# A perceiver layer on one core: the last 65 keys spread over four row groups, loaded by four transfers from ScalarE

## The chip, the core and the metric

The kernel runs on one core of a Trainium2 chip. Five engines work side by side: TensorE (PE; PEld is its weight load), VectorE (DVE), ScalarE (ACT), GpSimd (POOL) and SyncE (SP, which here only issues transfers). Each has a stream of its own, and they wait for each other by semaphores. Transfers issued on SP or on ScalarE are carried out by 16 DMA engines that all queues share. The metric is the device time of one execution in microseconds (us); lower is better.

## The reference, cut to what matters

The layer has three parts: cross-attention, a small self-attention, and a mixture of experts. The change touches the first alone. There are 32 batches with 64 queries each, a context of 1601 keys, and 256 channels, all in fp32.

```python
q = jnp.einsum('bsd,df->bsf', query, Wq) + bq       # query: x, normed; (32, 64, 256)
k = jnp.einsum('bsd,df->bsf', key_in, Wk) + bk      # key_in = value = ctx_1024; (32, 1601, 256)
v = jnp.einsum('bsd,df->bsf', value, Wv) + bv
attn = jnp.einsum('bqd,bkd->bqk', q, k)
probs = jax.nn.softmax(attn, axis=-1)
result = jnp.einsum('bqk,bkd->bqd', probs, v)
x = result + query                                  # then a layer norm with gamma and beta
```

## The kernel before, in words

The weights of queries and keys are multiplied ahead, so that scores come straight from the context. Two batches make a pair (128 query rows), and 16 pairs are worked through. The context of a pair lies in one of three slots of `ring`, as 12 chunks of 128 keys and a 13th chunk with the rest. 1601 is 12 x 128 + 65, and the 65 lie on partitions 0 to 64 of chunk 12 (`KT` is 12, `TAIL` 65, `Q` 32, `QUADS` 4).

For each pair VectorE turns the keys in blocks of 32 x 32 (L1714, eight column blocks of 128x832, into `ctxT`). Thus partitions 32a to 32a+31 hold the keys of row group a, for 32 channels. A row group's keys over the 13 chunks are `KW[a]` many: 416, 416, 385, 384. TensorE then makes the scores (`scores`, L1180): for each of 8 column blocks and 4 row groups and 2 batches a matmul with 32 rows, 64 columns and `KW[a]` moving columns, into bank a of `S`. An fp32 matmul leaves two records. VectorE takes the maximum over each bank (L1726), ScalarE the exponentials (`exps`, L901: five instructions, as `EXPS` lists the whole blocks of 32 and the odd column apart) with their sums. TensorE turns the probabilities chunk by chunk (`turn_probs`, L1194) in the parts `KPARTS`, chunks 0-3, 4-7, 8-11 and 12, into four banks; ScalarE copies each part (`turned_out`, L888); TensorE weighs the context with them (`weigh`, L1206).

In `turn(i)` TensorE does the scores of pair i, turns pair i-2's result, weighs pair i-1, projects pair i-2 and turns pair i's probabilities. ScalarE does the copies of pair i-1 first, then what belongs to pairs i-2 and i-3, then the exponentials of pair i. VectorE does the maxima of pair i, five column blocks of pair i+1, sums and residual, and the last three column blocks.

All loads of the context stand on SP (`load_part`, L439 for three transfers of four chunks, 1 MB each, L443 for the rest, 130 KB). `follow(i, r)` waits for the scores and, part by part, for the weighing of pair i-3, with a store of an older pair's result and the load of pair i's queries (`load_q`, L452) around it. VectorE begins a pair when all its transfers have landed (`ctx_loaded[r]`). ScalarE's own queue carries two loads of x, two bias vectors, and `store_q` (L861) three times. GpSimd zeroes chunk 12 of each slot at the start (`tails_ready`), and SP waits for it ahead of the first load. Bank 0 holds scores and then, from column 0 on, the first part of the turned probabilities.

Of the kernel before, what the change touches and what calls it, by code (L numbers as in the profile page):

```python
# [6 lines left out]
def perceiver_layer(nc, t, out):  # L7
# [9 lines left out]
    NL, NB, D = x_in.shape  # L17
# [64 lines left out]
    with cross:  # L82
# [85 lines left out]
        sums = sb("sums", [P, len(EXPS)])  # L168
# [258 lines left out]
        def _(sp):  # L427
# [6 lines left out]
            def load_part(i, r, g, loaded=None):  # L434

                pair = ctx_in[bass.ds(2 * i, 2)]
                ks = KPARTS[g]
                if ks[0] < KT:
                    sp.dma_start(ring[:, r, :, ks[0]:ks[-1] + 1, :].rearrange("p b k c -> p b (k c)"),  # L439
                                 pair[:, 0:KT * P, :].rearrange("b (p k) c -> p b k c", k=KT)[:, :, ks[0]:ks[-1] + 1, :]  # L440
                                 .rearrange("p b k c -> p b (k c)")).then_inc(loaded or ctx_loaded[r], 16)
# [30 lines left out]
            sp.wait_ge(tails_ready, RING)  # L472
# [342 lines left out]
        def _(act):  # L815
            for n in range(2):
                part = slice(*XPARTS[n])
                act.dma_start(x_all[:, part, :], x_rows[:, part, :]).then_inc(x_loaded[n], 16)
# [3 lines left out]
                          allow_slow_non_contiguous=True).then_inc(qkb_loaded, 16)  # L822
            act.wait_ge(wT_done, 1)
# [56 lines left out]
            queries_placed(0)  # L880
            queries_placed(1)

            def turned_out(i):

                for g, ks in enumerate(KPARTS):
                    rows = P if ks[0] < KT else TAIL
                    act.wait_ge(probT_done, i * len(KPARTS) + (g + 1))
                    act.copy(probT[0:rows, ks[0]:ks[-1] + 1, :].rearrange("p a b -> p (a b)"),  # L888
                             PT_BANKS[g][0:rows, 0:len(ks) * P]).then_inc(probT_copied, 1)

            def exps(i):
# [3 lines left out]
                for n, (a, lo, hi) in enumerate(EXPS):  # L895
                    if hi - lo >= Q:
                        to = by_slab[:, lo // Q:hi // Q, a, :]
                        of = S[a][:, lo:hi].rearrange("p (k j) -> p k j", j=Q)
                    else:
                        to, of = by_slab[:, lo // Q, a, 0:hi - lo], S[a][:, lo:hi]  # L900
                    act.activation(to, of, ACT.Exp, bias=negmax[:, 0:1], accum_out=sums[:, n:n + 1]).then_inc(exp_done, 1)  # L901
# [18 lines left out]
            def turn(i, ahead=True, back1=True, back2=True, back3=True, rows=None, queries=None):  # L920

                if back1:
                    turned_out(i - 1)
                if rows:
# [18 lines left out]
            turn(2, back3=False, queries=1)  # L943
            store_q(1)
            turn(3, rows=2)
            turn(4, queries=2)
            store_q(2)
            turn(5, rows=3)
            turn(6, queries=3)
            store_q(3)  # L950
            with act.Fori(7, PAIRS) as i:
                turn(i)
# [123 lines left out]
        def _(pe):  # L1076
# [107 lines left out]
            def turn_probs(i, first=False, turned=None):  # L1184

                pe.wait_ge(exp_done, (i + 1) * len(EXPS))
                for g, ks in enumerate(KPARTS):
# [4 lines left out]
                    for a, k in enumerate(ks):  # L1192
                        rows = P if k < KT else TAIL
                        last = pe.transpose(PT_BANKS[g][0:rows, a * P:a * P + P], prob[:, k * P:k * P + rows], ident[:, :])  # L1194
# [1059 lines left out]
```

## Time and profile before

| | |
|---|---|
| median of 3 runs | 530.31 us (527.97 to 533.57) |
| profiled execution | 530.5 us, span 528.3 us |
| TensorE busy | 493.6 us (93%) |
| VectorE busy | 387.4 us (73%) |
| ScalarE busy | 219.3 us (42%) |
| GpSimd busy | 203.6 us (39%) |
| granted TensorE clock | 0.985 of full speed |
| DMA moved | 108.92 MB, mean 206 GB/s |

The busy times say how long an engine had an instruction of its own running; DMA issues and waits are not in them. The attention stage is the first half of the span. The chain of waits follows the work back from the last instruction. The timeline lists instructions merged in groups, with the idle time ahead of a group in brackets and who ended it.

### The profile page before, as it was taken

How to read it: one execution, taken by the hardware profiler on the slowest of the kernel's cores; microseconds unless marked ns; L12 is line 12 of the kernel's file. 1: busy time of each engine (PE TensorE's matmuls, PEld its weight loads, DVE VectorE, ACT ScalarE, POOL GpSimd, SP SyncE). 2: the span in 40 equal slices, each digit the busy share in tenths (PEclk: the TensorE clock that was granted, in tenths of full speed). 3: DMA queues.
4: the chain of work that ended last, by engine and by line, in shares of the span. 5: the costliest groups of instructions: out<-in, count | busy, mean ns of one | idle time of the engine just before them, and what ended most of it. 6: DMA issues, size and time to landing. Idle time of an engine off the chain costs nothing.

```text
span 528.3 us, 14495 instructions
## 1 busy us (share of the span) xinstructions
PE 493.6 (93%) x5028; PEld 345.8 (65%) x5029; DVE 387.4 (73%) x1053; ACT 219.3 (42%) x656; POOL 203.6 (39%) x344
## 2 busy tenths in 40 slices
PE   7999999899999999999989999999988879999990
PEld 6766566565666666666655577767745658888870
DVE  4887896998788889898543588889776415555764
ACT  3344443353333434444331466656431025555510
POOL 5000422121222111222231577776676605566640
PEclk9999999999999999999999999999999979999996
DMA  7998979966989988884215999710122234555747
GB/s 287 358 342 296 224 229 301 330 212 176 323 293 299 308 292 285 292 270 133 58 41 154 274 321 299 206 51 2 45 88 82 90 100 143 164 160 149 231 107 232
DMA packets 67610, 108.92 MB, mean 206 GB/s; under 512 B 8371, under 2 KB 49381, under 8 KB 67560
## 3 DMA queue, kind: packets, MB, share of 16 engines
q1 hardware_dynamic: 60872, 97.57, 58.8%
q0 software_dynamic: 3792, 8.43, 4.6%
q10 hardware_dynamic: 2896, 2.23, 1.3%
q8 instruction: 33, 0.54, 0.5%
q14 instruction: 17, 0.14, 0.1%
HBM read 85.31 MB, written 24.85 MB: 209 GB/s over the span
## 4 chain that ended last, share of the span: by engine, by line
PE 75%; DVE 6%; DMA 6%; POOL 6%; issue 3%; ACT 2%; ACTq 1%; SPq 1%; POOLq 0%; DVEq 0%
PE banks L1206 16%; PE banks L1180 16%; PE banks L1590 8%; POOL rows_by_expert L773 4%; PE banks L1602 4%; PE banks L1194 3%; PE banks L1219 2%; DMA ring<-in_ctx_dram 2%; PE banks L1584 2%; PE banks L1317 2%; PE banks L1369 2%; PE banks L1227 2%; PE banks L1324 2%; PE banks L1340 1%; PE banks L1149 1%
## 5 line engine op out<-in xcount | busy, mean ns | idle before, releaser
L1714 DVE STREAM_TRANSPOSE ctxT<-ring 128x832 f32<-128x832 f32 x124 | 118.2, 1010 | 6.3 <-DMA ring<-in_ctx_dram 6.0
L1180 PE MATMUL banks<-ctxT,qT_all 32*64 32x416 f32 (+2 forms) x2048 | 94.4, 498 | 2.8 <-DVE ctxT L1714 1.5
L1206 PE MATMUL banks<-ring,prob 128*64 128x256 f32 (+1 forms) x832 | 93.6, 381 | 0.7 <-ACT prob L888 0.7
L1206 PEld LDWEIGHTS banks<-ring,prob 128*64 128x64 f32 (+1 forms) x832 | 58.7, 137 | 31.5 <-issue 4.2
L1180 PEld LDWEIGHTS banks<-ctxT,qT_all 32*64 32x64 f32 x2048 | 55.5, 131 | 33.1 <-issue 11.4
L672 POOL TENSOR_TENSOR var<-mv,eps 128x1 f32<-128x1 f32 x32 | 6.1, 191 | 147.6 <-DVE mv L1755 93.4
L807 POOL DMA_INDIRECT expert_out<-prob,dest x47 | 46.2, 983 | 41.1 <-issue 21.7
L1590 PE MATMUL banks<-ring,ctxT 128*128 x188 | 50.4, 392 | 0.1
L901 ACT ACTIVATE prob<-banks,negmax 128x416 f32<-128x416 f32 (+2 forms) x80 | 40.9, 531 | 19.8 <-DVE negmax L1736 19.8
L1726 DVE TENSOR_REDUCE blockmax<-banks 128x1 f32<-128x416 f32 (+1 forms) x64 | 32.3, 567 | 16.6 <-PE banks L1180 16.6
L720 POOL TENSOR_TENSOR ctxT<-ctxT,k_mask 128x1088 f32<-128x1088 f32 x16 | 33.1, 2068 | 24.9 <-ACT ctxT L997 24.9
L2169 DVE TENSOR_TENSOR ctxT<-banks,ctxT 128x128 f32<-128x128 f32 x47 | 13.7, 292 | 32.7 <-ACT ctxT L1058 32.5
L1590 PEld LDWEIGHTS banks<-ring,ctxT 128*128 128x128 f32 x188 | 33.3, 198 | 3.3 <-issue 0.5
L888 ACT COPY prob<-banks 128x512 f32<-128x512 f32 x64 | 27.5, 515 | 16.7 <-PE banks L1194 16.6
L1602 PE MATMUL banks<-ring,ctxT 128*128 x94 | 28.0, 381 | 0.0
L1194 PE MATMUL banks<-ident,prob 128*128 128x128 f32 (+1 forms) x208 | 25.6, 273 | 1.2 <-ACT turned L843 0.7
L918 ACT COPY UT<-banks 128x256 f32<-128x256 f32 x16 | 6.0, 374 | 48.8 <-PE banks L1213 48.8
L1194 PEld LDWEIGHTS banks<-ident,prob 128*128 128x128 f32 (+1 forms) x208 | 23.5, 140 | 3.3 <-ACT turned L843 1.0
L2176 DVE TENSOR_SCALAR prob<-banks,share 128x256 f32<-128x256 f32 x47 | 22.6, 480 | 1.5 <-PE banks L1602 0.8
L1058 ACT ACTIVATE ctxT<-banks 128x128 f32<-128x128 f32 x47 | 13.0, 277 | 23.5 <-PE banks L1590 23.5
L1584 PE MATMUL banks<-ident,ctxT 128*128 128x128 f32 x94 | 18.8, 285 | 3.7 <-DMA ctxT<-rows_by_expert 3.7
L691 POOL TENSOR_TENSOR xn_all<-xn_all,bv_b 128x256 f32<-128x256 f32 (+1 forms) x16 | 11.8, 738 | 22.3 <-DMA rbias_b<-n_L_ffn_router_bias_dram 20.5
(279 smaller groups left out, 947.6 us busy)
## 6 DMA issues: line engine op xcount, KB each, us to landing
ring<-in_ctx_dram SPq DMA_DIRECT2D x48, 1024.0 KB, 8.8
qT_all<-q_by_pair SPq DMA_DIRECT2D x56, 128.0 KB, 8.2
rows_by_expert<-blank SPq DMA_DIRECT2D x8, 774.0 KB, 5.8
ctxT<-rows_by_expert SPq DMA_DIRECT2D x47, 129.0 KB, 2.1
mid<-stage SPq DMA_DIRECT2D x30, 128.0 KB, 2.3
ring<-in_ctx_dram SPq DMA_DIRECT2D x16, 130.0 KB
ctxT<-mid SPq DMA_DIRECT2D x16, 128.0 KB, 3.5
qT_all<-mid SPq DMA_DIRECT2D x16, 128.0 KB, 4.4
```

Source lines behind the costliest of these rows:

```text
L720: pool.tensor_tensor(k_blk, k_T.unsqueeze(2).broadcast_to([P, GB, HEADS, NP]), k_mask[:, :].unsqueeze(1).unsqueeze(3).broadcast_to([P, GB, ...
L807: pool.indirect_dma_start(y_dram, bass.IndirectOffsetOnAxis(ap=dest[:, s:s + 1], axis=0), y_sb[:, r, :], None, bounds_check=TOPK * TOK - 1 ...
L888: act.copy(probT[0:rows, ks[0]:ks[-1] + 1, :].rearrange("p a b -> p (a b)"), PT_BANKS[g][0:rows, 0:len(ks) * P]).then_inc(probT_copied, 1)
L901: act.activation(to, of, ACT.Exp, bias=negmax[:, 0:1], accum_out=sums[:, n:n + 1]).then_inc(exp_done, 1)
L1180: last = pe.matmul(S[a][64 * b:64 * b + 64, 0:KW[a]], q_rep[mine, r, c, 64 * b:64 * b + 64], ctxT[mine, c, b, 0:KW[a]], start=c == 0, stop ...
L1194: last = pe.transpose(PT_BANKS[g][0:rows, a * P:a * P + P], prob[:, k * P:k * P + rows], ident[:, :])
L1206: last = pe.matmul(U[64 * b:64 * b + 64, 0:D], probT[0:rows, k, 64 * b:64 * b + 64], ring[0:rows, r, b, k, :], start=k == 0, stop=k == KT)
L1584: last = pe.transpose(bank[r % 2][:, dh * P:dh * P + P], row_in[:, r, dh * P:dh * P + P], ident[:, :])
L1590: last = pe.matmul(bank[2 + p][:, 0:2 * HID], rowT[:, p, k, :], w_gu[:, bass.ds(e, 1), k, :].squeeze(1), start=k == 0, stop=k == DH - 1)
L1602: pe.matmul(bank[6 + p][:, 0:D], hidT[:, p, :], w_down[:, bass.ds(e, 1), :].squeeze(1), start=True, stop=True)\
L1714: dve.transpose(ctxT[:, c].rearrange("p b (k j) -> p (b k) j", j=Q), ring[:, r].rearrange("p b k c -> p (b k) c")[:, :, columns(c):columns ...
L1726: dve.tensor_reduce(blockmax[:, a:a + 1], S[a][:, 0:KW[a]], AX.X, ALU.max).then_inc(blockmax_ready, 1)
```

## The change

The 65 keys of chunk 12 are spread 17, 16, 16, 16 over the four row groups (`TAILS`), each group's from partition 32a on, so that `KW` becomes 401, 400, 400, 400. Four transfers bring them, and they are issued on ScalarE by `load_rest`, one turn ahead of their use and behind the copies of `turned_out`. SP's four transfers now hold chunks 0-2, 3-6, 7-10 and 11. The exponentials become four, each over all 416 columns of its bank; the columns from `KW[a]` on hold -1e30, written once by VectorE, so their exponentials are zero. `KPARTS` becomes 3, 4, 4 and 2 chunks, which keeps the first part in bank 0 off these columns. The turned and weighed last chunk has 128 rows instead of 65. SP no longer waits for `tails_ready`; ScalarE does. The loop on ScalarE has three turns in its body instead of one.

```diff
-    KW = [KT * Q + max(0, min(Q, TAIL - Q * a)) for a in range(QUADS)]
-    EXPS = [(a, lo, hi) for a in range(QUADS) for lo, hi in ((0, KW[a] // Q * Q), (KW[a] // Q * Q, KW[a])) if lo < hi]
-    KG = 4
+    TAILS = [TAIL // QUADS + (1 if a < TAIL % QUADS else 0) for a in range(QUADS)]
+    KW = [KT * Q + n for n in TAILS]
+    NEVER = -1e30
...
-    KPARTS = [range(lo, min(lo + KG, KT + 1)) for lo in range(0, KT + 1, KG)]
+    KPARTS = [range(0, 3), range(3, 7), range(7, 11), range(11, KT + 1)]
+    CTX_LOADS = 16 * (len(KPARTS) + QUADS)
...
-                ks = KPARTS[g]
-                if ks[0] < KT:
-                    sp.dma_start(ring[:, r, :, ks[0]:ks[-1] + 1, :].rearrange("p b k c -> p b (k c)"),
...
-                else:
-                    sp.dma_start(ring[0:TAIL, r, :, KT, :],
-                                 pair[:, KT * P:KEYS, :].rearrange("b p c -> p b c")).then_inc(ctx_loaded[r], 16)
+                lo, hi = KPARTS[g][0], min(KPARTS[g][-1] + 1, KT)
+                sp.dma_start(ring[:, r, :, lo:hi, :].rearrange("p b k c -> p b (k c)"),
...
-            sp.wait_ge(tails_ready, RING)
...
+            def load_rest(i, r):
+
+                pair = ctx_in[bass.ds(2 * i, 2)]
+                for a, n in enumerate(TAILS):
+                    at = KT * P + sum(TAILS[:a])
+                    act.dma_start(ring[Q * a:Q * a + n, r, :, KT, :],
+                                  pair[:, at:at + n, :].rearrange("b p c -> p b c")).then_inc(ctx_loaded[r], 16)
...
+            act.wait_ge(tails_ready, RING)
+            load_rest(0, 0)
...
             queries_placed(0)
+            for i in range(1, RING):
+                load_rest(i, i)
             queries_placed(1)
...
-                for n, (a, lo, hi) in enumerate(EXPS):
...
+                for a in range(QUADS):
+                    act.activation(by_slab[:, :, a, :], S[a][:, 0:SLAB].rearrange("p (k j) -> p k j", j=Q), ACT.Exp,
+                                   bias=negmax[:, 0:1], accum_out=sums[:, a:a + 1]).then_inc(exp_done, 1)
...
                 if back1:
                     turned_out(i - 1)
+                if rest is not None:
+                    load_rest(i + 1, rest)
...
-            with act.Fori(7, PAIRS) as i:
-                turn(i)
+            turn(7, rest=2)
+            turn(8, rest=0)
+            with act.Fori(3, PAIRS // RING) as it:
+                for u in range(RING):
+                    turn(it * RING + u, rest=(u + 1) % RING)
+            turn(PAIRS - 1)
...
-            dve.wait_ge(ctx_loaded[0], 64)
+            dve.wait_ge(bk_row_copied, 1)
+            for a in range(QUADS):
+                dve.memset(S[a][:, KW[a]:SLAB], NEVER)
+            dve.wait_ge(ctx_loaded[0], CTX_LOADS)
             for c in range(SOONER):
                 chunks_turned(c, arrived, KT + 1).then_inc(block_ready, 1)
             for c in range(SOONER, BLOCKS):
                 block_turned(0, 0, c, 0)
-            dve.wait_ge(bk_row_copied, 1)
```

On ScalarE, one turn in the body of the loop stood like this before (`prob` is written in its second half, `probT`, by the copies; ISA and REGISTER_ALU set addresses and counts):

```order
L888 COPY prob<-banks 128x512
L887 REGISTER_ALU
L888 COPY prob<-banks 65x128
L918 COPY UT<-banks 128x256
L911 ISA
L912 ACTIVATE stage<-stage,nmr,rstd 128x16x16
L893 REGISTER_ALU
L901 ACTIVATE prob,sums<-banks,negmax 128x13x32 x2
L901 ACTIVATE prob,sums<-banks,negmax 128x12x32
L901 ACTIVATE prob,sums<-banks,negmax 128x1
L901 ACTIVATE prob,sums<-banks,negmax 128x12x32
```

The same place of the changed program, from the last copy on:

```order
L895 COPY prob<-banks 128x256
L817 ISA
L817 DMA ring<-in_ctx_dram 17x2x256
L817 ISA
L817 DMA ring<-in_ctx_dram 16x2x256
L817 ISA
L817 DMA ring<-in_ctx_dram 16x2x256
L817 ISA
L817 DMA ring<-in_ctx_dram 16x2x256
L921 COPY UT<-banks 128x256
L914 ISA
L915 ACTIVATE stage<-stage,nmr,rstd 128x16x16
```

Four transfers now stand between the last copy and the work on the older pairs.

On VectorE, the first keys of pair 0 stood like this before:

```order
L1698 COPY prob<-w_mem 128x2x128 x2
L1815 STREAM_TRANSPOSE ctxT<-ring 128x2x256 x4
L1815 STREAM_TRANSPOSE ctxT<-ring 128x2x160 x4
L1714 STREAM_TRANSPOSE ctxT<-ring 128x832 x4
L1784 ISA dotted,shift<-xn_all,bk_row 128x256
```

And in the changed program:

```order
L1705 COPY prob<-w_mem 128x2x128 x2
L1822 STREAM_TRANSPOSE ctxT<-ring 128x2x224 x4
L1831 MEMSET banks 128x15
L1831 MEMSET banks 128x16 x3
L1822 STREAM_TRANSPOSE ctxT<-ring 128x2x192 x4
L1721 STREAM_TRANSPOSE ctxT<-ring 128x832 x4
L1791 ISA dotted,shift<-xn_all,bk_row 128x256
```

The first step turns seven chunks instead of eight, four fills have come in behind it, and the second step turns six instead of five.

## Rows read from the trace of the kernel before

**Rows 1.** Window table, 180 to 210 us; columns as in its head.

```profile
core 0: us, PE busy (x) PEld busy (x) DVE busy (x) ACT busy (x) POOL busy (x), PEclk, DMA share, GB/s
180.00:210.00 30.00, 30.00 (x442) 20.12 (x434) 27.17 (x55) 11.91 (x34) 6.55 (x16) 1.00 0.87 285
```

**Rows 2.** Chain of waits, one steady turn: start us, us, what.

```profile
177.94 5.75 PE banks L1180 x112
...
184.06 5.77 PE banks L1206 x52
...
192.31 5.75 PE banks L1180 x112
```

**Rows 3.** Chain of waits, the first six pairs.

```profile
17.48 6.40 PE banks L1180 x113
...
28.05 2.55 ACT prob L901 x10
...
63.78 0.57 ACTq L861
...
65.11 0.59 ACT prob L888
...
80.31 12.46 DMA ring<-in_ctx_dram
```

**Rows 4.** Timeline of a steady turn: start, us, engine, line, operation, [idle before, releaser].

```profile
186.86 3.10 SPq L439 DMA_DIRECT2D ring<-in_ctx_dram  x3
...
188.28 0.26 ACT L901 ACTIVATE prob<-banks,negmax 128x1 f32<-128x1 f32 x1
...
188.52 0.59 ACT L901 ACTIVATE prob<-banks,negmax 128x384 f32<-128x384 f32 x1
...
190.27 0.36 SPq L443 DMA_DIRECT2D ring<-in_ctx_dram  x1
...
191.36 1.71 ACT L888 COPY prob<-banks 128x512 f32<-128x512 f32 x4 [1.01 <-PE banks L1194]
...
192.24 5.82 PE L1180 MATMUL banks<-ctxT,qT_all 32*64 32x416 f32 x128
...
193.20 2.88 DVE L1714 STREAM_TRANSPOSE ctxT<-ring 128x832 f32<-128x832 f32 x3
...
198.19 2.02 DVE L1726 TENSOR_REDUCE blockmax<-banks 128x1 f32<-128x416 f32 x4 [0.99 <-PE banks L1180]
...
198.46 0.37 ACT L918 COPY UT<-banks 128x256 f32<-128x256 f32 x1 [5.38 <-PE banks L1213]
...
200.94 4.75 DVE L1714 STREAM_TRANSPOSE ctxT<-ring 128x832 f32<-128x832 f32 x5
```

**Rows 5.** Groups by line and shape, 192 to 199 us: busy us, mean ns.

```profile
L1180 PE MATMUL banks<-ctxT,qT_all 32*64 32x416 f32 x64 | 5.8, 510 | 0.0
L1180 PE MATMUL banks<-ctxT,qT_all 32*64 32x385 f32 x32 | 5.4, 485 | 0.0
L1180 PE MATMUL banks<-ctxT,qT_all 32*64 32x384 f32 x32 | 5.4, 484 | 0.0
```

**Rows 6.** Timeline of the start.

```profile
1.32 0.46 SPq L429 DMA_DIRECT2D ring<-in_L_xattn_Wk_dram  x1
...
2.29 1.40 SPq L439 DMA_DIRECT2D ring<-in_ctx_dram  x3
...
11.12 0.29 DVE L1701 COPY bk_rep<-bk_col 128x256 f32<-128x256 f32 x1 [1.91 <-DMA bk_col<-in_L_xattn_bk_dram]
...
16.33 1.69 DVE L1815 STREAM_TRANSPOSE ctxT<-ring 128x320 f32<-128x320 f32 x4 [0.47 <-DMA ring<-in_ctx_dram]
```

**Rows 7.** DMA issues: KB each, median us from issue to landing.

```profile
mid<-stage SPq DMA_DIRECT2D x30, 128.0 KB, 2.3
...
q_by_pair<-w_mem ACTq DMA_DIRECT2D x8, 128.0 KB, 7.8
...
q_by_pair<-qT_all ACTq DMA_DIRECT2D x4, 128.0 KB, 8.3
```

**Rows 8.** Timeline of TensorE, the scores of pair 5.

```profile
104.29 2.78 PE L1180 MATMUL banks<-ctxT,qT_all 32*64 32x416 f32 x48 [1.54 <-DVE ctxT L1714]
```

More of the change, by code:

```diff
@@ L167, in perceiver_layer @@
         negmax = sb("negmax", [P, 1])
[L168 removed]
+        sums = sb("sums", [P, QUADS])
         rowsum = sb("rowsum", [P, 1])
@@ L436, in load_part @@
                 pair = ctx_in[bass.ds(2 * i, 2)]
[L437 to L444 removed]
+                lo, hi = KPARTS[g][0], min(KPARTS[g][-1] + 1, KT)
+                sp.dma_start(ring[:, r, :, lo:hi, :].rearrange("p b k c -> p b (k c)"),
+                             pair[:, 0:KT * P, :].rearrange("b (p k) c -> p b k c", k=KT)[:, :, lo:hi, :]
+                             .rearrange("p b k c -> p b (k c)")).then_inc(loaded or ctx_loaded[r], 16)
             def load(i, r):
@@ L885, in turned_out @@
                 for g, ks in enumerate(KPARTS):
-                    rows = P if ks[0] < KT else TAIL
                     act.wait_ge(probT_done, i * len(KPARTS) + (g + 1))
-                    act.copy(probT[0:rows, ks[0]:ks[-1] + 1, :].rearrange("p a b -> p (a b)"),
-                             PT_BANKS[g][0:rows, 0:len(ks) * P]).then_inc(probT_copied, 1)
+                    act.copy(probT[:, ks[0]:ks[-1] + 1, :].rearrange("p a b -> p (a b)"),
+                             PT_BANKS[g][:, 0:len(ks) * P]).then_inc(probT_copied, 1)
             def exps(i):
@@ L918, in UT_evac, with turn @@
                 act.copy(UT[:, :, :].rearrange("p a b -> p (a b)"), M[:, 0:D]).then_inc(UT_copied, 1)
-            def turn(i, ahead=True, back1=True, back2=True, back3=True, rows=None, queries=None):
+            def turn(i, ahead=True, back1=True, back2=True, back3=True, rows=None, queries=None, rest=None):
                 if back1:
                     turned_out(i - 1)
+                if rest is not None:
+                    load_rest(i + 1, rest)
                 if rows:
@@ L942, in _ @@
             rows_turned(1)
-            turn(2, back3=False, queries=1)
+            turn(2, back3=False, queries=1, rest=0)
             store_q(1)
-            turn(3, rows=2)
-            turn(4, queries=2)
+            turn(3, rows=2, rest=1)
+            turn(4, queries=2, rest=2)
             store_q(2)
-            turn(5, rows=3)
-            turn(6, queries=3)
+            turn(5, rows=3, rest=0)
+            turn(6, queries=3, rest=1)
             store_q(3)
-            with act.Fori(7, PAIRS) as i:
-                turn(i)
+            turn(7, rest=2)
[4 more added lines that the diff above has]
+            turn(PAIRS - 1)
             turn(PAIRS, ahead=False)
@@ L1192, in turn_probs @@
                     for a, k in enumerate(ks):
-                        rows = P if k < KT else TAIL
-                        last = pe.transpose(PT_BANKS[g][0:rows, a * P:a * P + P], prob[:, k * P:k * P + rows], ident[:, :])
+                        last = pe.transpose(PT_BANKS[g][:, a * P:a * P + P], prob[:, k * P:k * P + P], ident[:, :])
                     last.then_inc(probT_done, 1)
@@ L1203, in weigh @@
                     for k in ks:
-                        rows = P if k < KT else TAIL
                         for b in range(2):
-                            last = pe.matmul(U[64 * b:64 * b + 64, 0:D], probT[0:rows, k, 64 * b:64 * b + 64],
-                                             ring[0:rows, r, b, k, :], start=k == 0, stop=k == KT)
+                            last = pe.matmul(U[64 * b:64 * b + 64, 0:D], probT[:, k, 64 * b:64 * b + 64],
+                                             ring[:, r, b, k, :], start=k == 0, stop=k == KT)
                     last.then_inc(pv_done, 1)
```

12 lines of the change are left out of this document (3 added, 9 removed).

## The prediction, made before the changed kernel had run

> **What bounds the kernel now.** I read the window table first. In the middle of the attention stage TensorE is busy for 30.00 of 30.00 us, VectorE for 27.17, ScalarE for 11.91, and the DMA engines have a share of 0.87 [rows 1]. The chain of waits says the same: the scores of a pair (5.75 us) are followed by the weighing of the pair before (5.77), and the next scores begin 14.37 us after the last [rows 2]. So in this stretch a turn lasts as long as TensorE's own work, VectorE is 1.4 us per turn from being the bound, and the DMA is not far behind. Before the stretch the chain leaves TensorE: for one set of exponentials (2.55), for ScalarE's first copy after a turn (0.59), and at 80.31 for 12.46 us in which the keys of pair 5 arrive [rows 3].
>
> Next, one turn in order of time [rows 4]. Scores start at 192.24. ScalarE's copies of the turned probabilities end at 191.36 + 1.71 = 193.07; it then has nothing to do until 198.46. VectorE waits 0.99 us for the scores to end (198.19), makes the maximum, and at 200.94 turns the next pair's keys without a wait for DMA. That pair's large loads were issued on SP from 186.86 on.
>
> **The change part by part.**
>
> *Scores.* A row group works through its own matmuls beside the other three, so the widest group sets the pace. By the means, a 416-wide record takes 510 ns and a 384-wide one 484 [rows 5]: 26 ns for 32 columns, 0.81 ns a column. Each row group has two records after one another for each of 8 column blocks, and the widest goes from 416 to 401: 15 x 0.81 x 2 x 8 = 0.195 us per pair. Scaling 5.75 by 15/416 gives 0.207. I take 0.2. It counts where scores are on the chain: pairs 0 to 2, the last three of eight blocks of pair 5, pairs 6 to 15, 13.4 pairs, **-2.7**. Scores 3 and 4 lie ahead of the wait for pair 5's keys, which swallows what they gain.
>
> *Exponentials.* Five become four: the one-column step goes (188.28 to 188.52, 0.24 us [rows 4]), two grow by 32 columns (at 0.11 us for 128, as for the copies below, 0.03 each). ScalarE's exponentials are on the chain for pair 0 alone [rows 3]: **-0.2**. In the other turns ScalarE waits anyway.
>
> *The four parts of probabilities, 3, 4, 4 and 2 chunks instead of 4, 4, 4 and 1.* There are still four copies with the same columns in sum. The first shrinks from 512 to 384 columns; 512 take 0.59 us [rows 3], 256 take 0.37 [rows 4], so 0.11 less. It stands on the chain twice, behind the two stores of queries from ScalarE: **-0.2**. The 128 rows instead of 65 in the last turn and the last weighing cost nothing that I can see: the moving side keeps its 128 and 256 columns.
>
> *VectorE.* The maxima read 1601 columns before and after. The four fills of -1e30 stand at the start, where VectorE waits 0.47 us for keys [rows 6]: 4 x about 0.1 us, covered. The wait for the key bias, moved forward, is met by then, as TensorE has started on the direct queries. Uncovered, each would cost its length once.
>
> *The transfers.* Per pair, SP moves 11 + 1 chunks in four transfers instead of 12 in three plus the rest, and ScalarE issues four more. On ScalarE's queue an issue takes 0.57 us [rows 3]; four take 2.3, in an idle time of 5.38 us [rows 4], so they delay nothing on ScalarE. Here the change's price begins. The rest used to leave SP right behind the large loads, at 190.27, ten us ahead of its use. Now the same turn issues it after the copies, at 193.07, 193.6, 194.2 and 194.8, and VectorE cannot start the pair without all four. It wants them at 200.94 - 0.2 = 200.74, 5.9 us after the last issue. What does ScalarE's queue need? No row has such a load in this stretch, so I bound it. Below: 128 KB written by SP in a quiet moment lands after 2.3 us [rows 7], in time with 3.6 us over. Above: the two kinds of ScalarE transfers of this stage, whose packets share the engines with SP's loads, land after 7.8 and 8.3 us [rows 7]; from the last issue that is 202.6 to 203.1, 1.9 to 2.4 late. These carry 128 KB each and ours 34, but the surroundings are theirs: SP's queue is loading keys and then queries, and the share of all engines is 0.87. I take a landing 7.1 us after the last issue, nearer the upper end: **1.2 us late**.
>
> What does lateness cost? VectorE has 0.99 us idle ahead of the maxima [rows 4], 0.8 once scores are 0.2 shorter. TensorE wants the last of the eight column blocks at 192.24 + 7 x 5.75 / 8 = 197.3 and VectorE has it at 193.20 + 2.88 = 196.1, 1.2 us sooner; with blocks of 5.55 / 8 it is 1.0. So about the first 0.9 us are free, and what is over comes out of the turn: 0.3. Turns 7 to 14 have this shape (earlier ones are longer, because of the queries' matmuls; the last loads nothing): 8 x 0.3 = **+2.4**. Behind VectorE stands more: its first norm of an older pair feeds a store that SP does ahead of its loads, and so the next keys. This would amplify lateness, which is why I keep the upper end.
>
> *The start.* SP no longer waits for the zeroing, so its first keys leave at 1.8 instead of 2.29 [rows 6], 0.5 us sooner. Against this the rest of pair 0 now stands on ScalarE's queue behind the bias vectors, of which one landed at about 11.1 [rows 6], and pair 0's keys were used at 16.33. With SP's queue full, ScalarE's part should end at or somewhat after that; pair 1 the same. VectorE paces these first scores. I put **+0.6**, bounds -0.2 and +2.
>
> Sum: -2.7 - 0.2 - 0.2 + 2.4 + 0.6 = -0.1. The profiled execution took 530.5 us (span 528.3), the median of the runs 530.31, so 530.4 there is **530.2** as a median.
>
> The Trainium skill has a rule that speaks against this change, in "DMA: Bandwidth & Descriptors", section "Why a DMA increments its semaphore by 16 and not by 1": a transfer is split over the largest number of engines up to 16 that divides its outer dimension. By it, 17 rows run on one engine and 16 rows on sixteen, where the 65 rows ran on thirteen. No row of the profile shows a 17-row transfer; what it would do is the third rival.
>
> **The rivals.** *The rest arrives in time* (0.28). For it: only 130 KB, and other small transfers land in 2.3 us [rows 7]. Against it: those of ScalarE's queue never did under load. Then +2.4 and +0.6 go: 530.3 - 3.1 = 527.2.
>
> *In time, and pair 5 gains as well* (0.07). The keys of pair 5 end with the rest, at the tail of SP's queue, and TensorE stands 1.54 us for them [rows 8]. If the rest is off that queue and early, this goes too: 527.2 - 1.5 = 525.7, and with the slower pace around it up to 1 us less. Against it: the bytes are the same and still share the engines.
>
> *One engine carries the first of the four* (0.15; the side slower than before). An engine moves 285 / 16 / 0.87 = 20.5 GB/s [rows 1], 50 ns for 1 KB and 200 for 4 KB. If all 34 packets of the 17-row transfer are on one engine and alternate with SP's 4 KB packets, they take 34 x 0.25 = 8.5 us while SP's queue is full, against 2 packets of each 16-row transfer. Issued at 193.07, with 2 us until it moves and SP's queue empty for the last part of it, this lands at about 202.7, 2.0 late, 1.1 over the slack: 8 x 1.1 = +8.8, and 530.3 - 3.1 + 0.6 + 8.8 = 536.6. It decides from a landing 6.8 us after the last issue (0.9 late). That is where the rule of the skill would lead.
>
> *The narrower groups do not shorten the scores* (0.05). Were the pace set by the number of instructions, -2.7 would vanish: 532.9. Against it: the means follow the width [rows 5].
>
> **How the numbers follow.** The forecast as worked out has 0.45. It is a balance of a gain of 3.1 and a loss of 3.0, and the loss may be anything from 0 to 9. The range 525.8 to 535.6 leaves out half of the second and most of the third rival. About 1% (5.3 us) is what a measurement of this kernel can tell from no change: faster by more 0.08, slower by more 0.14, within it 0.78.
>
> **What would show it.** Right: scores at 5.55 instead of 5.75; the exponentials four times 0.58; in the steady turns a wait of VectorE's key transposes on a DMA of ring, 0.5 to 1.5 us each, and turns of 14.3 to 14.6 us. If that wait is absent and turns are 14.16, the first rival holds; if it is over 1.5 and turns are over 14.8, the third. Wrong altogether: a wait of ScalarE's copies behind its own issues, or scores that still take 5.75.

## The result, and the profile after

The changed kernel took **538.61 us** (median of 4 runs, 537.93 to 539.73) against 531.94 for the kernel before on the same chip (4 runs, 527.97 to 533.94). The ratio is 1.0139, 95% interval [1.0099, 1.0179]: slower by 1.4%. The prediction said 530.2, within 525.8 to 535.6, so the time lies outside its range, on the side of its third rival. Ratios here and below leave out executions in a slower state of the chip, which is one reason why a ratio can differ a little from that of two medians.

The profiled execution took 537.93 us (span 535.7; before 528.3). Each profile shows one execution; this one is the fastest of the four, with the highest mean clock (0.986; the others 0.975 to 0.981). Two groups of its page, by line: the transposes of keys and the scores (busy us, mean ns of one, idle time before and its releaser):

```profile
L1721 DVE STREAM_TRANSPOSE ctxT<-ring 128x832 f32<-128x832 f32 x124 | 118.2, 1009 | 17.1 <-DMA ring<-in_ctx_dram 17.0
L1189 PE MATMUL banks<-ctxT,qT_all 32*64 32x400 f32 (+1 forms) x2048 | 98.1, 508 | 5.7 <-DVE ctxT L1721 4.4
```

The mean of the scores' records, 508 ns, does not show the gain: a 416-wide record took 510 before [rows 5], and several scores of the changed kernel are stretched (6.15 to 6.27 us in the chain below). The gain shows in undisturbed scores, 5.56 us instead of 5.75.

VectorE's transposes of keys wait 17.0 us for transfers into the ring of keys, 11 times; the same group of the kernel before waited 6.0 us, three times. Two of those, from VectorE's timeline of the kernel before (keys of pairs 3 and 5):

```profile
56.67 4.75 DVE L1714 STREAM_TRANSPOSE ctxT<-ring 128x832 f32<-128x832 f32 x5 [1.00 <-DMA ring<-in_ctx_dram]
...
92.87 4.75 DVE L1714 STREAM_TRANSPOSE ctxT<-ring 128x832 f32<-128x832 f32 x5 [3.33 <-DMA ring<-in_ctx_dram]
```

The waits of the changed kernel in order of time (61.67 is for pair 3, 97.19 for pair 5, 150.53 for pair 8):

```profile
17.80 1.96 DVE L1822 STREAM_TRANSPOSE ctxT<-ring 128x384 f32<-128x384 f32 x4 [0.92 <-DMA ring<-in_ctx_dram]
...
29.85 7.53 DVE L1721 STREAM_TRANSPOSE ctxT<-ring 128x832 f32<-128x832 f32 x8 [1.18 <-DMA ring<-in_ctx_dram]
...
61.67 4.75 DVE L1721 STREAM_TRANSPOSE ctxT<-ring 128x832 f32<-128x832 f32 x5 [4.33 <-DMA ring<-in_ctx_dram]
...
97.19 4.75 DVE L1721 STREAM_TRANSPOSE ctxT<-ring 128x832 f32<-128x832 f32 x5 [1.92 <-DMA ring<-in_ctx_dram]
...
150.53 4.75 DVE L1721 STREAM_TRANSPOSE ctxT<-ring 128x832 f32<-128x832 f32 x5 [2.66 <-DMA ring<-in_ctx_dram]
...
194.60 4.75 DVE L1721 STREAM_TRANSPOSE ctxT<-ring 128x832 f32<-128x832 f32 x5 [0.80 <-DMA ring<-in_ctx_dram]
...
209.49 1.97 DVE L1721 STREAM_TRANSPOSE ctxT<-ring 128x832 f32<-128x832 f32 x2 [1.05 <-DMA ring<-in_ctx_dram]
```

The chain of waits (start us, us, what) shows where the time is lost. First the kernel before, three rows that were not shown yet, then the changed one:

```profile
32.29 5.75 PE banks L1180 x113
...
116.56 5.75 PE banks L1180 x113
...
249.75 5.75 PE banks L1180 x111
```

```profile
2.39 9.93 DMA bk_col<-in_L_xattn_bk_dram
...
18.64 5.88 PE banks L1189 x120
...
34.24 5.56 PE banks L1189 x125
...
50.24 11.33 DMA ring<-in_ctx_dram
...
120.88 6.15 PE banks L1189 x125
...
171.19 8.63 DMA ring<-in_ctx_dram
...
199.57 5.58 PE banks L1189 x124
...
213.76 6.27 PE banks L1189 x125
...
228.64 6.25 PE banks L1189 x126
...
243.50 5.73 PE banks L1189 x124
...
257.84 5.56 PE banks L1189 x124
```

Read the start of a pair's scores as a clock. Taking before from after, it runs late by

| scores of pair | before | after | late | what lies between |
|---|---|---|---|---|
| 0 | 17.48 [rows 3] | 18.64 | 1.2 | key bias lands late |
| 1 | 32.29 | 34.24 | 2.0 | pair 0's keys late as well, 0.92 us at 17.80; scores paced by VectorE |
| 6 | 116.56 | 120.88 | 4.3 | the wait of 4.33 us at 61.67; that at 97.19 is shorter than before's 3.33 |
| 11 | 192.31 [rows 2] | 199.57 | 7.3 | waits of 2.66 at 150.53 and 1.94 at 179.84 |
| 15 | 249.75 | 257.84 | 8.1 | four steady turns |

Half of the lateness is there by pair 6, ahead of the turns 7 to 14 that the prediction took as alike, and nine tenths by pair 11. From pair 11 to pair 15 the turns take 14.19, 14.88, 14.86 and 14.34 us, 14.57 in the mean against 14.36 before.

### The profile page after: what moved, and what is told of

It reads as the page before. It is cut to its first block, busy times and chain, and to the rows that moved or that the text cites. A ratio compares the mean times of both kernels' runs of the same rounds, so it can differ in the third digit from the quotient of the medians.

```text
span 535.7 us, 14540 instructions
## 1 busy us (share of the span) xinstructions
PE 497.6 (93%) x5028; PEld 331.4 (62%) x5029; DVE 390.7 (73%) x1057; ACT 218.0 (41%) x624; POOL 203.4 (38%) x344
## 4 chain that ended last, share of the span: by engine, by line
PE 63%; DMA 13%; DVE 10%; POOL 6%; issue 4%; ACT 2%; ACTq 1%; SPq 0%; DVEq 0%; POOLq 0%
PE banks L1213 13%; PE banks L1189 11%; PE banks L1597 8%; DMA ring<-in_ctx_dram 7%; POOL rows_by_expert L769 4%; DVE ctxT L1721 4%; PE banks L1609 4%; PE banks L1202 2%; PE banks L1226 2%; PE banks L1591 2%; DMA bk_col<-in_L_xattn_bk_dram 2%; PE banks L1324 2%; PE banks L1234 2%; PE banks L1331 2%; PE banks L1347 1%
## 5 line engine op out<-in xcount | busy, mean ns | idle before, releaser
L1189 PE MATMUL banks<-ctxT,qT_all 32*64 32x400 f32 (+1 forms) x2048 | 98.1, 508 | 5.7 <-DVE ctxT L1721 4.4
L1213 PE MATMUL banks<-ring,prob 128*64 128x256 f32 x832 | 93.5, 381 | 0.7 <-ACT prob L895 0.7
L1213 PEld LDWEIGHTS banks<-ring,prob 128*64 128x64 f32 x832 | 58.5, 137 | 31.5 <-issue 4.2
L1189 PEld LDWEIGHTS banks<-ctxT,qT_all 32*64 32x64 f32 x2048 | 40.8, 132 | 54.2 <-issue 30.6
L903 ACT ACTIVATE prob<-banks,negmax 128x416 f32<-128x416 f32 x64 | 37.9, 608 | 17.3 <-DVE negmax L1743 17.3
L1733 DVE TENSOR_REDUCE blockmax<-banks 128x1 f32<-128x401 f32 (+1 forms) x64 | 32.3, 566 | 10.5 <-PE banks L1189 10.5
L895 ACT COPY prob<-banks 128x384 f32<-128x384 f32 (+1 forms) x64 | 28.5, 514 | 15.3 <-PE banks L1202 15.3
L1202 PE MATMUL banks<-ident,prob 128*128 128x128 f32 x208 | 25.6, 273 | 1.1 <-ACT turned L849 0.8
L1202 PEld LDWEIGHTS banks<-ident,prob 128*128 128x128 f32 x208 | 23.6, 141 | 3.2 <-ACT turned L849 1.1
```

The costliest lines, as they stand in the source:

```text
L895: act.copy(probT[:, ks[0]:ks[-1] + 1, :].rearrange("p a b -> p (a b)"), PT_BANKS[g][:, 0:len(ks) * P]).then_inc(probT_copied, 1)
L903: act.activation(by_slab[:, :, a, :], S[a][:, 0:SLAB].rearrange("p (k j) -> p k j", j=Q), ACT.Exp, bias=negmax[:, 0:1], accum_out=sums[:, ...
L1189: last = pe.matmul(S[a][64 * b:64 * b + 64, 0:KW[a]], q_rep[mine, r, c, 64 * b:64 * b + 64], ctxT[mine, c, b, 0:KW[a]], start=c == 0, stop ...
L1202: last = pe.transpose(PT_BANKS[g][:, a * P:a * P + P], prob[:, k * P:k * P + P], ident[:, :])
L1213: last = pe.matmul(U[64 * b:64 * b + 64, 0:D], probT[:, k, 64 * b:64 * b + 64], ring[:, r, b, k, :], start=k == 0, stop=k == KT)
L1733: dve.tensor_reduce(blockmax[:, a:a + 1], S[a][:, 0:KW[a]], AX.X, ALU.max).then_inc(blockmax_ready, 1)
```

## The experiments

Two suspects, and a rival to each. **A**: the transfer of 17 rows is carried by one DMA engine and lands last. Its rival **B**: the rest is late because ScalarE issues it late, or because its queue is slow, whatever the number of rows. **S**: at the start, the removed wait of SP lets the large key loads go out earlier, and the small loads behind which the first scores stand (the key bias) land later. Its rival: the four transfers behind the bias on ScalarE's own queue do it.

**1. 18, 16, 16 and 15 keys instead of 17, 16, 16 and 16.** Only the table of row counts changes; the widest group grows by one column.

```diff
-    TAILS = [TAIL // QUADS + (1 if a < TAIL % QUADS else 0) for a in range(QUADS)]
+    TAILS = [18, 16, 16, 15]
```

> The 65 keys lie 18, 16, 16, 15 over the row groups instead of 17, 16, 16, 16; all else, the queue, the moment of issue and the number of transfers, is as in the changed kernel. Theory A, one engine carries all 34 packets of the 17-row transfer: 18 rows divide over more engines (4 packets on each of nine), so VectorE's waits for ring fall from 17.0 us to under 7 and the time from 538.6 to 527 to 531. Theory B, the transfers leave too late and on the wrong queue: the waits stay at 15 us or more, the time at 537 to 540.

Measured: 533.82 us, ratio 1.0055 [1.0019, 1.009]; the profiled span is 530.7, 5.0 less than that of the changed kernel. The waits for keys halve, to 8.5 us, and most steady turns are 14.16 us long (one of the last four is 14.37), which is the full gain that the prediction gave to the scores. Part of the shorter waits is due to a later start, which gives the first keys more time; runs 5 and 7 below compare 18 rows with 17 at nearly the same start, 12.2 us against 18.7. From the chain of waits:

```profile
2.40 10.51 DMA bk_col<-in_L_xattn_bk_dram
...
15.87 6.59 PE banks L1158 x32
22.47 5.55 PE banks L1189 x114
...
196.12 5.55 PE banks L1189 x112
...
210.28 5.55 PE banks L1189 x113
```

The time still missed what A expected, as did the waits (under 7 us). The rows show what else is lost: the key bias lands at 12.9, TensorE stands for it, and then the 32 matmuls of the direct queries (L1158) take 6.59 us where the same 32 take 3.67 in the changed kernel. The window table gives the granted clock third from the end, of the changed kernel first, then of this one:

```profile
15.00:30.00 15.00, 14.18 (x192) 9.83 (x191) 10.56 (x26) 6.19 (x18) 0.00 (x0) 1.00 1.06 359
```

```profile
15.00:30.00 15.00, 15.00 (x183) 11.83 (x184) 10.21 (x24) 4.59 (x13) 0.00 (x0) 0.77 1.05 371
```

1.00 is the upper level of 2.4 GHz; a mean of 0.77 says that for part of these 15 us TensorE ran at 1.2 GHz. Pair 0's scores begin at 22.47, 5.0 us later than before.

**2. 17, 17, 17 and 14 keys.** The opposite test of A: three transfers of 17 rows per pair, with the same widest group.

```diff
-    TAILS = [TAIL // QUADS + (1 if a < TAIL % QUADS else 0) for a in range(QUADS)]
+    TAILS = [17, 17, 17, 14]
```

> The keys lie 17, 17, 17, 14: three transfers of 17 rows in place of one, the same bytes and packets in sum. Theory A: 102 packets on the same engine instead of 34, 3.4 us or more later per pair under load, and the time goes up by at least 20 us, to 560 or more. Theory B, and any theory that looks at bytes, queue or moment: no change, 537 to 541.

Measured: 566.89 us (a single execution, span 564.7), as A expected. The waits for keys are 36.5 us, and ScalarE is held by its own issues; from the chain of waits:

```profile
3.87 5.38 ACTq L817
9.29 3.84 ACTq L817
...
27.59 7.27 ACTq L817
```

The 64 issues of these transfers have a median of 0.34 us and a longest of 1.33 in the changed kernel; here three take 5.38, 3.84 and 7.27. Nothing but row counts differs from the changed kernel, so B alone cannot make these 28 us.

The packets say the same more directly. ScalarE's queue is q10 on the pages (packets, MB, share): the kernel before, the changed one, run 1, run 2.

```profile
q10 hardware_dynamic: 2896, 2.23, 1.3%
...
q10 hardware_dynamic: 5760, 4.36, 2.9%
...
q10 hardware_dynamic: 5872, 4.36, 2.9%
...
q10 hardware_dynamic: 5248, 4.36, 2.4%
```

Over the kernel before these are 179, 186 and 147 packets more for each of the 16 pairs. 130 of them are the rows of 1 KB; the others, 49, 56 and 17, are packets of 4 bytes. 49 is 1 + 16 + 16 + 16, 56 is 9 + 16 + 16 + 15, 17 is 1 + 1 + 1 + 14: as many as there would be with one small packet from each engine that a transfer runs on. Both runs and these counts agree with the rule of the Trainium skill that the prediction cited ("DMA: Bandwidth & Descriptors", section "Why a DMA increments its semaphore by 16 and not by 1"), by which 17 rows go to one engine and 16 or 18 rows to many. The times of the small packets show what it costs: for pair 3 of the changed kernel 45 of the 49 have gone by 55.1 us, the last four only between 59.7 and 60.8, so one engine ends 5.7 us behind all the others. In run 1 the 56 of the same pair follow each other without such a gap up to 58.7.

**3. The kernel before, its one transfer of 65 rows issued from ScalarE a turn ahead.** B alone: late issue and ScalarE's queue, without the split.

```diff
-                else:
-                    sp.dma_start(ring[0:TAIL, r, :, KT, :],
-                                 pair[:, KT * P:KEYS, :].rearrange("b p c -> p b c")).then_inc(ctx_loaded[r], 16)
...
+            def load_rest(i, r):
+
+                pair = ctx_in[bass.ds(2 * i, 2)]
+                act.dma_start(ring[0:TAIL, r, :, KT, :],
+                              pair[:, KT * P:KEYS, :].rearrange("b p c -> p b c")).then_inc(ctx_loaded[r], 16)
```

> The kernel before with one step of the change alone: its one 65-row transfer of the rest is issued on ScalarE, a turn ahead, behind the copies, at the places of the changed kernel. Theory A: 65 rows run on many engines, it lands in time in the steady turns, 529 to 533 (the start may lose up to 1 us). Theory B: the steady turns wait for ring as in the changed kernel, at 14.7 us or more per turn, 536 to 541.

Measured: 535.47 us, ratio 1.0044 [1.0004, 1.0084], between the times that A (529 to 533) and B (536 to 541) expected; the rows decide. Only three waits for keys are left, 4.1 us in sum, none over 0.3 us in the steady turns from pair 9 on. Its queue has 143 packets more per pair, 13 of them small. B falls for the steady turns: the rest, issued late and from ScalarE, is in time when it is spread over 13 engines. For the first pairs the run says less, as pair 0's scores begin 7.1 us late (24.63), which gives their keys time. What is lost is again at the start, where the bias is waited for 4.22 us and the granted clock is 0.70 from 15 to 30 us; the removed wait of SP is in this kernel too.

**4. The changed kernel, its four transfers issued by SP behind the large loads.** This tells whether the 17-row transfer hurts on either queue, and whether the bias is held up by what stands behind it on ScalarE's.

```diff
+                load_rest(i, r)
...
+            sp.wait_ge(tails_ready, RING)
+            load_rest(0, 0)
...
-            act.wait_ge(tails_ready, RING)
-            load_rest(0, 0)
...
-            for i in range(1, RING):
-                load_rest(i, i)
```

> The changed kernel with its four transfers of the rest (17, 16, 16, 16 rows) back on SP, behind the fourth large load of the pair. Theory A: the 34 packets still run on one engine, but behind the large loads and not in alternation with them, about 2 us later than the rest of the pair, ten us ahead of use in the steady turns; small waits at pairs 0 to 5, 527 to 533. Theory B: full recovery and the gain of the scores, 526 to 529.

Measured: 536.52 us, ratio 1.0114 [1.0066, 1.0162], waits for keys 12.3 us; by time it cannot be told from the changed kernel, and it is above what either theory expected (527 to 533, 526 to 529). From VectorE's timeline, the copy of the key bias and the wait for pair 3's keys:

```profile
12.34 0.29 DVE L1706 COPY bk_rep<-bk_col 128x256 f32<-128x256 f32 x1 [3.13 <-DMA bk_col<-in_L_xattn_bk_dram]
...
59.97 2.90 DVE L1719 STREAM_TRANSPOSE ctxT<-ring 128x832 f32<-128x832 f32 x3 [3.17 <-DMA ring<-in_ctx_dram]
```

The copy waits as long as in the changed kernel (12.35, 3.14 us), though nothing stands behind the bias on ScalarE's queue now. So the four transfers are not what holds it. And pair 3's keys, waited for 3.17 us here, 4.33 in the changed kernel and 0.46 in run 1 (1.15 in run 5, whose start is in time), are late on SP's queue too if 17 rows are among them: A, not the queue.

**5. 18, 16, 16, 15 with SP's wait put back.**

```diff
+            sp.wait_ge(tails_ready, RING)
             for g in range(len(KPARTS)):
                 load_part(0, 0, g, ctx_first if g < 2 else None)
```

> The kernel of e1_18 with one line put back: SP waits for the zeroing before its first load, as in the kernel before. Theory S: without that wait SP's megabytes of keys stand ahead of the last small loads, the bias vectors land over 1 us later, TensorE waits at the start and can lose its clock for some us. Then this lands the bias by 11.3, starts the scores of pair 0 near 17.5, and takes 527 to 530.5, under e1_18 by 3 us or more. Rival: the bias is late because ScalarE's four transfers follow it on its own queue; then nothing changes, 532 to 535.

Measured: 532.46 us, ratio 0.9986 [0.9946, 1.0025]. The copy of the bias waits 1.72 us, the clock from 15 to 30 us is 1.00 again, and pair 0's scores begin at 18.12. So the mechanism at the start is S, not its rival. The time is not S's (527 to 530.5) but lies in the rival's range: the waits for keys grew to 12.2 us, and in the profiled executions all that the start gave back was spent there, as pair 15's scores begin at 253.13, and at 252.97 in run 1.

**6. The kernel before without that wait** (only the 65-row transfer still waits for the zeroing).

```diff
-            sp.wait_ge(tails_ready, RING)
             for g in range(len(KPARTS)):
+                if g == len(KPARTS) - 1:
+                    sp.wait_ge(tails_ready, RING)
                 load_part(0, 0, g, ctx_first if g < 2 else None)
```

> The kernel before with that one step of the change alone: SP's first three large loads go out without waiting for the zeroing (the rest of pair 0 still waits). ScalarE's queue is as before. Theory S: the bias lands at 12 or later, scores of pair 0 start 1 us or more later, and the time is 1 to 5 us over the kernel before. Rival: as before, within 1 us, or 0.5 us better by the earlier keys.

Measured: 535.58 us, ratio 1.0058 [1.0023, 1.0094]. From the chain of waits:

```profile
2.40 11.13 DMA bk_col<-in_L_xattn_bk_dram
...
16.69 6.42 PE banks L1150 x32
23.10 5.75 PE banks L1181 x114
```

This is S by itself, in a kernel that has nothing else of the change: the large key loads leave SP sooner, the bias lands at 13.5 instead of 11.1 [rows 6], the direct queries take 6.42 us, and pair 0's scores begin at 23.10 instead of 17.48 [rows 3]. Removing the wait costs 0.6% (0.2 to 0.9).

**7. The changed kernel with SP's wait put back.**

> The changed kernel (17, 16, 16, 16) with that line alone put back. By theory A its waits for ring stay at about 15 us and the turns at 14.7; by theory S its start is 1 to 4 us sooner. Together 534 to 537. If the start did not matter: 538 to 539.

The edit is that of run 5, on the changed kernel. Measured: 538.58 us, ratio 1.0128 [1.0052, 1.0204], no gain to be seen and above the 534 to 537 expected. The bias is waited for 2.46 us, pair 0's scores begin at 18.41, but the waits for keys rise from 17.0 to 18.7 us. So in this execution the earlier start is given back at the key loads that follow. With runs 1 and 5 this makes a square:

| | SP's wait removed | SP's wait in place |
|---|---|---|
| 17, 16, 16, 16 | 538.61, 1.0139 [1.0099, 1.0179] | 538.58, 1.0128 [1.0052, 1.0204] |
| 18, 16, 16, 15 | 533.82, 1.0055 [1.0019, 1.009] | 532.46, 0.9986 [0.9946, 1.0025] |

One row moved from a group of 16 into that of 17 is worth 4.8 us by the medians in one column and 6.1 in the other, and 4.5 and 7.6 us by the ratios, which compare better across the chips that the runs were on. What the wait is worth is less clear. By the ratios it is 0.7% in the lower row, but 1.4 us by the medians and nothing by pair 15 in the profiled executions; in the upper row the interval is too wide to tell.

With SP's wait in place the starts are nearly alike, so the waits for keys of a pair (us) can be compared:

| keys of pair | before | 17 rows (run 7) | 18 rows (run 5) | 18 rows, on SP (run 8) |
|---|---|---|---|---|
| 1 | 1.68 | 2.09 | 1.15 | 0.16 |
| 3 | 1.00 | 3.82 | 1.15 | 1.71 |
| 5 | 3.33 | 3.23 | 4.47 | 4.49 |
| 7 | 0 | 1.78 | 0.99 | 0 |
| 8 | 0 | 2.63 | 2.38 | 1.02 |
| 10 to 14 | 0 | 5.12 | 2.07 | 0.83 |
| sum | 6.0 | 18.7 | 12.2 | 8.2 |

Most of what 17 rows cost is at pair 3 and in the steady turns. The wait for pair 8 is there with 18 rows as well. In that turn four stores of queries stand ahead of the rest on ScalarE's queue (issued from 136.69 on, the rest from 139.16, in the changed kernel), which is the likely reason, though no run takes them away. So a part of B holds, a small one.

**8. 18, 16, 16, 15, the wait in place, the four transfers on SP behind the large ones.** What is left of the change is the narrower groups, the four exponentials, the parts of 3, 4, 4 and 2 chunks with the loads cut to match, and the fills; the rest still comes in four transfers.

> Rows 18, 16, 16, 15, the wait on SP put back, and the four small transfers on SP behind the large ones instead of on ScalarE. If both causes are as theories A and S say, this keeps the scores' 3 us and has no late rest in the turns behind the stores of queries: 526.5 to 529.5, at or under e6_18_wait. If four small transfers in SP's queue cost as much there: 530 to 533.

Measured: **530.96 us**, ratio 0.9967 [0.9936, 0.9997], the best of all and only just clear of no change. The time lies in the second of the two ranges, in which four small transfers cost on SP's queue too. From its chain of waits and VectorE's timeline:

```profile
17.74 5.65 PE banks L1187 x110
...
83.20 10.38 DMA ring<-in_ctx_dram
...
118.74 5.55 PE banks L1187 x116
...
251.29 5.55 PE banks L1187 x111
```

```profile
93.68 4.75 DVE L1719 STREAM_TRANSPOSE ctxT<-ring 128x832 f32<-128x832 f32 x5 [4.49 <-DMA ring<-in_ctx_dram]
```

The start is that of the kernel before, within 0.3 us. Pair 6 is 2.2 us late (118.74 against 116.56), behind a wait of 4.49 us for the keys of pair 5, where the kernel before waits 3.33; pair 15 is 1.5 us late in this execution. The scores do gain their 0.2 us a pair, but ahead of the wait for pair 5's keys the gain is lost and a little more.

**9 to 11. The two bias vectors loaded ahead of x.** If the bias is late because it stands behind two transfers of x on ScalarE's queue, put it ahead. The same edit in three kernels: run 8 as it is; run 8 with SP's wait moved to just ahead of the small transfers; and the changed kernel.

```diff
+            act.dma_start(bq_col[:, :], t["L0_xattn_bq"].rearrange("(k p) -> p k", p=P),
+                          allow_slow_non_contiguous=True).then_inc(qkb_loaded, 16)
+            act.dma_start(bk_col[:, :], t["L0_xattn_bk"].rearrange("(k p) -> p k", p=P),
+                          allow_slow_non_contiguous=True).then_inc(qkb_loaded, 16)
             for n in range(2):
                 part = slice(*XPARTS[n])
                 act.dma_start(x_all[:, part, :], x_rows[:, part, :]).then_inc(x_loaded[n], 16)
```

> The kernel with tails of 18, 16, 16, 15 keys on SP and SP's first wait in place (930.96 us is not its time: it took 530.96, ratio 0.9967), with one edit: ScalarE issues the two bias columns ahead of the two transfers of x rather than behind them. Theory S (the bias column's landing sets when TensorE scores pair 0; bk_rep waits 1.90 us for it there): the wait falls below 0.7 us, scores of pair 0 begin 0.5 to 1.5 us earlier, time 529 to 530.5, unless x, now two issues later, holds VectorE instead. Rival (the 1.9 us are not on the path, or x pays for them): no change, 530.5 to 531.5, with the wait moved to x_all.

> The same as the run before it with SP's first wait moved from ahead of its large key loads to just ahead of the small ones, so that the large loads start as early as in the changed kernel. Theory S (early key loads cost only because the bias columns, queued behind x, then land late): with the bias ahead of x the wait of bk_rep stays under 1.5 us, TensorE's granted clock doesn't fall in 15 to 30 us, and the time is within 0.5 us of the run before it (529 to 530.5). Rival (the early key loads slow everything that is loaded at the start, x and the query weights too, wherever the bias stands): 532 to 535, with idle time of VectorE or TensorE for x or weights before 20 us.

> The changed kernel with that one edit alone (bias columns ahead of x on ScalarE's queue; 17, 16, 16, 16 keys, ScalarE issues the rest). Theory S with A: the start's share (bk_rep's wait 3.14 us, scores of pair 0 1.2 us late and 1 us longer) goes, the 17-row transfer's waits stay at 15 to 19 us: 535.5 to 537.5 against its 538.6. If the waits for the 17-row transfer swallow what the start gives back, as with SP's wait put back: 538 to 539.

Measured: 538.27 us, 1.0094 [1.006, 1.0128]; 542.42 us, 1.0185 [1.0147, 1.0222]; 545.78 us, 1.0251 [1.0216, 1.0286]. They are 8, 12 and 8 us above what theory S expected. The chain of waits of the first, and below it a row of VectorE's timeline of run 8, where x stands first:

```profile
2.40 9.58 DMA x_all<-in_x_dram
12.01 0.75 DVE x_stats L1663 x2
...
20.61 5.47 PE banks L1156 x32
26.08 5.55 PE banks L1187 x111
```

```profile
6.01 0.75 DVE L1663 BATCH_NORM_STATS2 x_stats<-x_all 128x6 f32<-128x256 f32 x2 [0.49 <-DMA x_all<-in_x_dram]
```

The statistics of the second part of x begin at 12.01 instead of 6.01. Two transfers of 1 KB each, made of single elements, hold the 512 KB behind them up by 6 us, 1.1 of them because x is issued at 1.88 instead of 0.82, and the direct queries follow. In the second and third kernel, where SP's keys go out early as well, x is waited for up to 6.4 us at a time. So the order on ScalarE's queue was right as it was. Of the second kernel the rival held in kind (early key loads slow x too, wherever the bias stands): it is 4.2 us slower than the first, and both are far above the times named. Of the third kernel neither reading held.

**12. Run 8 with chunks 7 to 11 in one transfer.** Is the wait for pair 5's keys made by the lone chunk, which moves in packets of 1 KB?

```diff
+    LPARTS = [range(0, 3), range(3, 7), range(7, KT)]
...
-                lo, hi = KPARTS[g][0], min(KPARTS[g][-1] + 1, KT)
+                lo, hi = LPARTS[g][0], LPARTS[g][-1] + 1
```

> The kernel with tails of 18, 16, 16, 15 keys on SP behind the large loads and SP's first wait in place (530.96 us, ratio 0.9967), with chunks 7 to 11 loaded by one transfer of 1280 KB instead of one of 1024 KB and one of 256 KB (1 KB runs per row). It starts only when the pair's last chunk has been weighed. Theory P (what is left of the waits for keys, 8.2 us in five waits with 4.5 for pair 5, comes from the packets of 1 KB of the lone chunk, 4 times as many per byte as in the 1024 KB transfers): ring waits fall to 4 to 6 us and the time to 528 to 530. Rival (those waits come from the bytes in flight and the stores of queries that share the queues, not from the size of packets): ring waits 7 to 10 us, 530 to 532.

Measured: 533.29 us where the kernel before took 536.13 beside it, ratio 0.997 [0.9934, 1.0005], and waits for keys of 7.1 us in a profiled execution of 540.7, of which 5.5 for pair 5. That is run 8's ratio (0.9967) and no better. The lone chunk's packets are gone and that wait is not shorter, so nothing speaks for their size as its cause; but the merged transfer also starts later, which could hide a gain. What makes the wait is open: the stores of queries, the four more transfers per pair and the order of the first loads were not separated.

## Why the prediction was wrong

**Scores, -2.7: right per pair, wrong in the sum.** Undisturbed scores take 5.55 us against 5.75, and turns with waits under 0.5 us take 14.16 (run 1), as worked out. But the sum counted pairs 0 to 2 and 6 to 10 as gains. In the changed kernel those lie ahead of waits for keys, at 61.67, 150.53 and 179.84, which swallow them. The prediction had said so of pairs 3 and 4, ahead of pair 5's wait, and had not asked where new waits of this kind would stand.

**Exponentials and copies, -0.4: right in kind.** In the chain four exponentials take 2.37 us for pair 0, instead of 2.55 for five.

**Issues on ScalarE: near enough.** They take 0.34 us each in the median (0.25 to 1.33) instead of 0.57. From the timeline of ScalarE's queue, a steady turn of the changed kernel, then of run 1 (18 rows), each with the transposes that wait for what was issued:

```profile
199.77 0.26 ACTq L817 DMA_DIRECT2D ring<-in_ctx_dram  x1
...
200.48 1.32 ACTq L817 DMA_DIRECT2D ring<-in_ctx_dram  x3
```

```profile
197.12 1.35 ACTq L817 DMA_DIRECT2D ring<-in_ctx_dram  x3
...
204.85 1.97 DVE L1721 STREAM_TRANSPOSE ctxT<-ring 128x832 f32<-128x832 f32 x2 [0.26 <-DMA ring<-in_ctx_dram]
```

**The late rest, +2.4: this is the step that failed, and mostly by its scope.** In run 1 the rest is there 204.85 - 198.47 = 6.4 us after the last issue ended, and in the changed kernel 209.49 - 201.80 = 7.7. The prediction took 7.1 counted from the start of the last issue, where the two would be some 6.8 and 8.1, so it was 1.0 short. In the steady turns that matters little: 14.57 - 14.16 = 0.41 us a turn instead of 0.3. The loss is elsewhere. The term was worked out for one steady turn, times the turns 7 to 14, and two of those are not steady: 2.66 us for pair 8 in turn 7, 1.94 for pair 10 in turn 9. Ahead of them stands pair 3 with 4.33 us, for which the prediction had no term at all; 1.00 of it was there before, and 1.15 is left with 18 rows and the start in time (run 5). There the one engine of the 17-row transfer ends 5.7 us behind the others. Pair 8's wait has another cause for the most part, since 18 rows on ScalarE's queue wait 2.32 to 2.38 us there too; the stores of queries ahead of them are the likely one. The whole price of the 17-row transfer is what the square shows: 4.5 to 7.6 us.

**The third rival had the mechanism, and its time came near by luck.** It said one engine, 536.6 us, with 15% given to it; the time was 538.6. Its sum was not right: 2.0 us late in each steady turn, 8 times 1.1, where the turns showed 0.41. The waits outside the steady turns, which it left out, made up for that. The prediction had the rule of the Trainium skill in hand and gave it 15% because no row showed a 17-row transfer. No row spoke against it either; the bounds taken for the late rest (2.3 and 8.3 us to land) were both from transfers with a row count that is a multiple of 16 (128 and 32), and so could not bound a case of one engine.

**The start, +0.6: its first half had the wrong sign.** SP's keys leaving sooner was booked as a gain of 0.5 us. Run 6 shows that this alone costs 0.6%, and its profile shows the way: a late bias and a TensorE clock of 0.77. In the profiled execution of the changed kernel the clock did not fall, and pair 0's scores are 1.2 us late and pair 1's 2.0, the latter in part by late keys; what the clock did in its other executions, which had a lower mean, no trace shows. The bias vector was in the rows that the prediction quoted, waited for 1.91 us [rows 6]: a transfer on the path, which the edit put behind more traffic. The reason given for a loss, that the rest stands behind the bias on ScalarE's queue, was not the cause (run 4).

**What would show it.** The test that the prediction wrote down (waits over 1.5 us and turns over 14.8 for the third rival) would have decided wrongly or not at all: the waits of the last four turns were 0.50 to 1.05 us and the turns 14.57 in the mean, inside the bounds of its forecast, while single turns reached 14.88 and the waits in turns 7 and 9 were over 1.5. It looked at a stretch where the cause shows least. The counts of packets on ScalarE's queue decide at once.

## What to carry to other kernels

Choose the row counts of a split transfer before its width: 17, 16, 16, 16 cost 4.5 to 7.6 us more here than 18, 16, 16, 15, which costs one column of width. When a transfer gets later or slower, price it where its queue is fullest and at the first waits of the stage, not in the steady turn alone, and ask which gains lie ahead of such a wait. A wait at the start that seems idle may be holding traffic back from a small load on the critical path: look for the smallest transfer that the first work waits for.

## What the runs showed of the hardware

A transfer's rows decide over how many engines it goes: the counts of small packets fit 1, 9, 16, 15, 14 and 13 engines for 17, 18, 16, 15, 14 and 65 rows (49, 56, 17 and 13 packets a pair in the changed kernel and runs 1 to 3). The one engine of a 17-row transfer ended 5.7 us behind the others at pair 3. Several such transfers can block the issuing engine: with three per pair an issue on ScalarE took up to 7.27 us, with one per pair at most 1.33. A vector of 256 single elements is expensive to whatever stands behind it: two of them delayed 512 KB of x by 6 us, while at the end of the queue the second lands 8.7 us after issue (2.41 to 11.1 in run 8) and 11.13 us in run 6, where the key loads leave sooner. And a late landing at the start can cost more than itself: the same 32 matmuls took 3.67 to 3.69 us where VectorE had waited 1.4 to 3.1 us for the bias (runs 4, 5, 7, 8, 12 and both kernels), and 6.42 to 6.60 (runs 1, 3 and 6) where it had waited 3.7 to 4.35 and TensorE stood behind it, with a mean granted clock of 0.70 to 0.77 from 15 to 30 us. In run 2 it waited 4.10 us, but these matmuls came later (22.78), and took 3.69.
